# Cross attention with 16 heads over 1500 keys: spreading the reciprocal denominators by TensorE in every batch

## The reference, cut to what matters

```python
scores = einsum('bshd,bld->bhsl', q_latent, kv_r)   # 16 batches, 56 x 16 rows, 1500 keys
attn   = softmax(scores, axis=-1)
ctx_c  = einsum('bhsl,bld->bhsd', attn, kv_r)       # latent width 64
out    = folded_output_projection(ctx_c)
```

## Time and profile before

| | |
|---|---|
| device time, median of 3 executions | 3199.64 us |
| lowest and highest | 3179.69 and 3200.17 us |
| span of the profiled execution, first to last instruction | 3214.1 us |
| cross attention of layer 0, layer 1, layer 2 | 226 to 652, 1327 to 1751, 2300 to 2719 us of the span |

### The profile page before, as it was taken

How to read it: one execution, slowest core, us unless ns; L and a number is a source line. 1 busy time by engine, 2 the same in 40 slices (tenths; PEclk the granted TensorE clock), 3 DMA queues, 4 the chain that set the end, 5 groups by cost and what they waited for, 6 DMA issues and landing times. The chain is left out here.

```text
span 3214.1 us, 48214 instructions
## 1 busy us (share of the span) xinstructions
PE 2927.4 (91%) x17993; PEld 1703.9 (53%) x17997; DVE 1876.2 (58%) x3657; ACT 1245.7 (39%) x1997; POOL 873.8 (27%) x743
## 2 busy tenths in 40 slices
PE   4899999869999899899999989989899999677999
PEld 3755555545455463455556557753455555346444
DVE  6568888642222357778875143347788885654222
ACT  3456666511111242555554122222456554424221
POOL 4325555400343124333333000004333333211000
PEclk8899999979999899999999999999999999888999
DMA  1148898614122112377775010012367775001111
GB/s 32 53 124 179 177 181 172 135 29 134 35 105 92 52 43 78 88 152 171 168 148 138 11 42 25 26 43 78 77 154 165 153 167 134 15 12 24 39 40 33
DMA packets 221444, 299.25 MB, mean 93 GB/s; under 512 B 127178, under 2 KB 149052, under 8 KB 218764
## 3 DMA queue, kind: packets, MB, share of 16 engines
q1 hardware_dynamic: 220348, 294.39, 39.2%
q10 hardware_dynamic: 864, 1.77, 0.2%
HBM read 120.52 MB, written 21.38 MB: 44 GB/s over the span
## 5 line engine op out<-in xcount | busy, mean ns | idle before, releaser
L1796 ACT ACTIVATE l2x_shared<-l2x_shared,l2x_a_low 128x1500 f32<-128x1500 f32 x112 | 173.3, 1547 | 160.4 <-DVE l2x_shared L1748 156.5
L1796 ACT ACTIVATE l1x_shared<-l1x_shared,l1x_a_low 128x1500 f32<-128x1500 f32 x112 | 173.3, 1548 | 159.6 <-DVE l1x_shared L1748 156.1
L1796 ACT ACTIVATE l0x_shared<-l0x_shared,l0x_a_low 128x1500 f32<-128x1500 f32 x112 | 173.3, 1548 | 146.4 <-DVE l0x_shared L1748 145.7
L1660 PE MATMUL l0x_a_S_ps<-l0x_kt,l0x_a_q 64*128 64x366 f32 (+1 forms) x896 | 176.0, 507 | 3.5 <-DVE l0x_shared L1748 3.0
L1660 PE MATMUL l1x_a_S_ps<-l1x_kt,l1x_a_q 64*128 64x366 f32 (+1 forms) x896 | 178.6, 515 | 0.6 <-DVE l1x_shared L1748 0.6
L1660 PE MATMUL l2x_a_S_ps<-l2x_kt,l2x_a_q 64*128 64x366 f32 (+1 forms) x896 | 178.4, 515 | 0.6 <-DVE l2x_shared L1748 0.6
L2040 DVE TENSOR_TENSOR l0f_times_up<-l0f_gate,l0f_U 128x448 f32<-128x448 f32 x64 | 39.8, 621 | 236.9 <-PE l0f_U L1958 236.9
L2009 ACT ACTIVATE l0f_gate<-l0f_G 128x448 f32<-128x448 f32 x72 | 39.2, 545 | 310.7 <-PE l0f_G L1953 310.7
L1353 POOL TENSOR_TENSOR l2x_q_straight<-l2x_q_straight,l2x_q_crossed 128x448 f32<-128x448 f32 x48 | 54.5, 1136 | 339.6 <-DVE l2x_q_crossed L1344 339.6
L1695 PE MATMUL l1x_a_C_ps<-l1x_space,l1x_v 128*64 128x192 f32 (+1 forms) x1024 | 121.8, 373 | 21.7 <-DMA l1x_space<-l1x_a_blocks 18.9
L1695 PE MATMUL l2x_a_C_ps<-l2x_space,l2x_v 128*64 128x192 f32 (+1 forms) x1024 | 117.8, 363 | 20.8 <-DMA l2x_space<-l2x_a_blocks 17.2
(11 more groups left out here) (678 smaller groups left out, 6478.7 us busy)
## 6 DMA issues: line engine op xcount, KB each, us to landing
l0x_space<-normed SPq DMA_DIRECT2D x192, 128.0 KB
l1x_space<-normed SPq DMA_DIRECT2D x192, 128.0 KB
l2x_space<-normed SPq DMA_DIRECT2D x192, 128.0 KB
l0x_space<-l0x_a_blocks SPq DMA_DIRECT2D x186, 96.0 KB, 3.3
l1x_space<-l1x_a_blocks SPq DMA_DIRECT2D x186, 96.0 KB, 3.3
l2x_space<-l2x_a_blocks SPq DMA_DIRECT2D x186, 96.0 KB, 3.4
l0f_gu<-in_L_ffn_gu SPq DMA_DIRECT2D x36, 256.0 KB, 2.6
l0x_a_q<-l0x_qa SPq DMA_DIRECT2D x32, 224.0 KB
```

Of the source, the lines that this page charges most:

```text
L1660: last = pe.matmul(S_ps[:, 2 * pair + rows_, 0:w], q[lane, b % 2, k * 128:(k + 1) * 128], kt[lane, b % 2, pair * W1:pair * W1 + w], start= ...
L1796: act.activation(p[:, n % 2], p[:, n % 2], ACT.Exp, bias=low[:, n % 2, 1:2], scale=-1.0, accum_out=den[:, b % 2, k:k + 1]).then_inc(exp_re ...
```

## The change

The path through DRAM is gone, and every batch is normalised as the last one was. PE makes the 14 products at the ends of groups 0 and 1 of every batch; DVE multiplies `cn` in place, after tile k = 3 (group 0) and after tile k = 6 (group 1) of the next batch; POOL's scatter is a copy that waits for both; SP neither stores nor loads inverses. PE waits, before it starts a group of the next batch in its bank, until DVE has read the reciprocals out of it.

```diff
-                    if b > 0:
-                        fetch_inverses(b - 1)
...
                     move(sp, b, 1, range(4) if b + 1 < B else range(2))
-                    if b + 1 < B:
-                        store_inverses(b)
...
                 def scatter(b):
                     pool.wait_ge(kept_own, 8 * b + 12 if b + 1 < B else 8 * B)
-                    if b + 1 == B:
-                        pool.wait_ge(normed, 2)
-                        pool.tensor_copy(ct[:, :, b, 0:S], cn[:, b % 2].rearrange("c (s h) -> c h s", s=S)).then_inc(scattered, 1)
-                        return
-                    pool.wait_ge(c_kept, 2 * b + 2)
-                    pool.wait_ge(r_loaded[b % 2], 32 * (b // 2 + 1))
-                    pool.tensor_tensor(ct[:, :, b, 0:S], cn[:, b % 2].rearrange("c (s h) -> c h s", s=S),
-                                       rrow[:, b % 2].rearrange("c (s h) -> c h s", s=S), ALU.mult).then_inc(scattered, 1)
+                    pool.wait_ge(normed, 2 * b + 2)
+                    pool.tensor_copy(ct[:, :, b, 0:S], cn[:, b % 2].rearrange("c (s h) -> c h s", s=S)).then_inc(scattered, 1)
...
                         if b > 0:
                             pe.wait_ge(c_kept, 2 * (b - 1) + g + 1)
+                            pe.wait_ge(normed, 2 * (b - 1) + g + 1)
...
-                    if b + 1 == B:
-                        pe.wait_ge(rden_ready, B)
-                        for t in range(COUNT[g]):
...
+                    pe.wait_ge(rden_ready, b + 1)
+                    for t in range(COUNT[g]):
+                        k = FIRST[g] + t
+                        for odd in range(2):
+                            last = pe.matmul(C_ps[odd * CW:(odd + 1) * CW, g, 256 + t * 64:320 + t * 64],
+                                             rden[:, b % 2, k:k + 1].to_broadcast([128, CW]),
+                                             m.ident[:, odd * CW:(odd + 1) * CW], start=True, stop=True)
                     last.then_inc(valued, 1)
...
                 def invert(b):
 
                     if b > 1:
-                        dve.wait_ge(r_stored[b % 2], 16 * (b // 2))
+                        dve.wait_ge(valued, 2 * (b - 2) + 2)
                     dve.reciprocal(rden[:, b % 2], den[:, b % 2]).then_inc(rden_ready, 1)
...
                     if n + 2 < N:
                         negate(n + 2)
-                normalise(0)
-                normalise(1)
+                    if n % T in (3, 6) and n >= T:
+                        normalise(n // T - 1, n % T // 6)
+                normalise(B - 1, 0)
+                normalise(B - 1, 1)
```

More of the change, by code:

```diff
@@ L1440, in attend @@
     cn = ahead.shared[:, 2 * LK:2 * LK + C].rearrange("c (a n) -> c a n", a=2)
-    rrow = ahead.shared[:, 2 * LK + C:2 * LK + 2 * C].rearrange("c (a n) -> c a n", a=2)
     def group(k):
@@ L1478, in attend @@
         c_kept = st.sem(name + "c_kept")
-        r_stored = [st.sem(f"{name}r_stored{j}") for j in range(2)]
-        r_loaded = [st.sem(f"{name}r_loaded{j}") for j in range(2)]
         normed = st.sem(name + "normed")
@@ L1522, in store_keys @@
                     sp.dma_start(m.kt_dram[b], kt[:, b % 2]).then_inc(k_stored[b % 2], 16)
[L1524 to L1539, removed]
                 for b in range(2):
@@ L1768, in invert, with normalise @@
                     if b > 1:
-                        dve.wait_ge(r_stored[b % 2], 16 * (b // 2))
+                        dve.wait_ge(valued, 2 * (b - 2) + 2)
                     dve.reciprocal(rden[:, b % 2], den[:, b % 2]).then_inc(rden_ready, 1)
-                def normalise(g):
-                    b = B - 1
+                def normalise(b, g):
                     a, z = columns(g)
@@ L1858, in latent_cross @@
         m.kt_dram = nc.dram_tensor("kt_rotated", (B, 128, LK // 2), F32, kind="Internal").ap()
-        m.r_dram = nc.dram_tensor("inverses", (B, QT_TILES, 128), F32, kind="Internal").ap()
         ctx = d["ctx"], d["ctx_cos"], d["ctx_sin"]
```

## The result

Over twelve executions of each kernel the median is 3166.29 us, against 3191.97 us before. The ratio is 0.992, 95% interval 0.990 to 0.9941: 0.8% faster. Each kernel had one disturbed execution among its twelve (3478.8 us before, 3373.5 us after), which the medians hold and the ratio leaves out. The first three of the twelve executions of the kernel before had a median of 3199.64; all twelve together lie lower, and the other eleven spread from 3174.65 to 3205.99, while those of the changed kernel keep within 3157 and 3170.

A forecast was written before the change was run, and what follows sets the result against it. TensorE was taken to bound the steady loop, with irregular DMA waits besides. Profiled: 3214.1 + 49.5 (products) - 60 (relief) - 4 (last batches) = 3199.6 us; timed, the middle between 3185 and about 3200 gave 3193, range 3168 to 3230.

The forecast's parts named there:

- What bounds the kernel: Cross attention: TensorE is full in undisturbed batches (24.76 us in layer 1); late DMA moves add an irregular 71.1 us together.
- the price of the products: Ends of groups 0 and 1 on PE: 0.63 and 0.47 us, 1.10 us a batch, +49.5 us over 45 batches.
- wrong it would be if the undisturbed batch isn't 25.9 us: Sign in the profile after: undisturbed windows of layers 1 and 2 should last 25.86 us with PE full.
- The relief: PE's waits for moves and slow clock shrink: -60 us (bounds 35 and 71), with -4 us more in the last batches.
- The discount for timed executions: Profiled span against timed median: 14.5 us of delays may be missing in timed executions; the middle of both cases was taken.
- rival 2: All DMA delays go, the last batches' waits too: 3199.6 + 49.5 - 71 - 11 = 3167 us; chance 0.12.
- The cause: SP's store of inverses: small DRAM writes hold up transfers next to them; 3.5 KB took over 11 us to land.
- SP's queue: Without the two loads, 1.34 us of queue go, so moves of group 1 start at 1572.25 instead of 1573.59.
- The slack of 0.63 us: Group 0's products precede the tile needing the moves; with 1.34 us of queue, a late move has 2.0 us more.
- Rival 1: Moves stay late and products are paid: 3249 us without relief, 3226 with the 2 us of slack; chance 0.21.
- rival 4: VectorE becomes the bound through its two multiplications: up to +40 us, 3233 us; chance 0.04.
- Rival 3: Products run slower in PE's stream, 0.10 us a record: +126 us in place of +49.5, 3262 us; chance 0.03.

The follow-up runs named there:

- experiment 1: Changed kernel without the 14 products in batches 1 to 14 of each stage: 3131.4 us, ratio to the kernel before 0.9725.
- experiment 2: Changed kernel with the store of inverses in 4 B pieces put back behind the moves of group 1, read by nobody: 3191.0 us, ratio to the kernel before 0.9913.
- experiment 4: Changed kernel with the store put back at its old place as 128 pieces of 28 B, read by nobody: 3170.6 us, ratio to the kernel before 0.9845.
- experiment 5: Changed kernel with the 4 B store put back directly in front of the moves of group 0: 3230.9 us, ratio to the kernel before 1.0095.
- experiment 9: Changed kernel with the 4 B store back and two small loads of 7 rows of 512 B in the old loads' place: 3181.9 us, ratio 0.9941.
- experiment 8: Changed kernel with store and loads of inverses both back at their old places, read by nobody: 3206.6 us, ratio to the kernel before 1.0008.
- experiment 3: Changed kernel with both loads of inverses put back in every batch, the store only in each stage's first two batches: 3175.7 us, ratio 0.9869.

## Why the prediction missed

**What bounds the kernel** was right: a steady loop bound by TensorE, and an irregular cost from the moves. The forecast of a full PE in every batch, no wait for `normed`, DVE below PE and moves of group 1 issued earlier came true. DVE is busy 22.78 us in a batch of 25.58. POOL idles 9.7 us before its copy, in place of 12.5 before its multiplication; the copy comes right behind DVE's multiplication. The moves of group 1 start 1.4 us after the turn of tile k = 6 begins:

```profile
1528.84 0.35 DVE L1745 TENSOR_TENSOR l1x_shared<-l1x_shared,l1x_a_C_ps 128x192 f32<-128x192 f32 x1
...
1529.32 1.01 POOL L1578 COPY l1x_ct<-l1x_shared 128x448 f32<-128x448 f32 x1 [9.70 <-DVE l1x_shared L1745]
...
1550.85 0.70 PE L1643 MATMUL l1x_a_T_ps<-ident,l1x_shared 128*119 128x128 f32 x4
...
1552.23 1.18 SPq L1502 DMA_DIRECT2D l1x_space<-l1x_a_blocks  x2
```

In the kernel before the same turn began at 1570.37, and these moves 3.2 us after it, at 1573.59:

```profile
1570.37 0.70 PE L1673 MATMUL l1x_a_T_ps<-ident,l1x_shared 128*119 128x128 f32 x4
```

So they come 1.8 us earlier, where 1.3 was forecast.

**The step that failed is the price of the products**: "less than that I exclude". I read 0.63 us from the start of their loads to the start of the next loads, and took the next piece to be unchanged behind them. It isn't. The end of group 0 in the changed kernel:

```profile
1537.97 0.63 PEld L1666 LDWEIGHTS l1x_a_C_ps<-l1x_space,l1x_v 128*64 128x64 f32 x8 [0.51 <-issue]
...
1538.67 0.71 PEld L1677 LDWEIGHTS l1x_a_C_ps<-ident,l1x_a_rden 128*64 128x64 f32 x16
1538.88 0.64 PE L1677 MATMUL l1x_a_C_ps<-ident,l1x_a_rden 128*64 128x64 f32 x16
1539.29 0.20 PEld L1664 LDWEIGHTS l1x_a_C_ps<-l1x_space,l1x_v 119*64 119x64 f32 x4
...
1539.77 0.50 PEld L1643 LDWEIGHTS l1x_a_T_ps<-ident,l1x_shared 128*119 128x119 f32 x4 [0.28 <-issue]
```

and the same place in the kernel before:

```profile
1558.30 0.63 PEld L1695 LDWEIGHTS l1x_a_C_ps<-l1x_space,l1x_v 128*64 128x64 f32 x8 [0.51 <-issue]
...
1559.00 0.36 PEld L1693 LDWEIGHTS l1x_a_C_ps<-l1x_space,l1x_v 119*64 119x64 f32 x4
...
1559.64 0.50 PEld L1673 LDWEIGHTS l1x_a_T_ps<-ident,l1x_shared 128*119 128x119 f32 x4 [0.28 <-issue]
```

The products take their 0.62 us, from 1538.67 to 1539.29. But the four loads behind them take 0.20 us in place of 0.36, and the next turn comes 0.48 us after these loads began in place of 0.64: 0.16 us are given back. So group 0 costs 1.80 - 1.34 = 0.46 us from the first row to the last, group 1 by the windows 0.82 - 0.46 = 0.36, and 45 batches 36.9 us in place of 49.5. The prediction had named the sign itself: wrong it would be if the undisturbed batch isn't 25.9 us. It is 25.58.

**The relief** was sized at 60 + 4 us. Against the profiled execution all went: the span fell by 53.7 us with 36.9 us added, so 90.6 us of waits and slow clock are gone, 71.1 in the windows and 19.5 in the first and last batches and outside, where the prediction had put 4 for the last batches, and 11 at most. The medians give less: 25.7 + 36.9 = 62.6 us. The discount for timed executions was thus right in kind, and rival 2 (everything goes) is what happened in the profile. Its 3167 is the measured time within 1 us, but by luck: the products were 12.6 us cheaper than in its sum and the three executions it starts from 7.7 us too slow, and against that the medians gave 62.6 us of relief in place of its 82. With 36.9 for the products alone it would have been 3155.

The miss of 26.7 us against the forecast of 3193 is made up of 12.6 us for the products, 7.7 us by which the median of twelve executions of the kernel before is below that of three, and 6.4 us of relief (62.6, where the forecast had 3199.6 + 49.5 - 3193 = 56.1). The time lies only 2 us under the range, so without any one of the three it would have been inside. The products are the largest part, and the one that both the windows and experiment 1 show.

**The cause** I gave for the late moves was the store's small writes, as a reading that the trace didn't prove. Experiments 2, 4 and 5 show it for the part that the store plays: the same bytes in 28 B pieces cost 4 us, in 4 B pieces 25 us, and in 4 B pieces just ahead of other moves 65 us. What the prediction took as speaking against it, that the late move was issued before the store, is no objection: the late move is the store's direct neighbour in the queue, as the landings beside experiment 5 show. But it isn't the store alone: with the loads beside it, it costs more than both by themselves. By SP's queue, as the prediction had it (1.34 us earlier), nothing was won that experiment 9 could find, with about half of that time put back. The slack of 0.63 us in front of PE's use is there in the order of the work, and experiment 8 fits it; it would have saved some 20 us there, which wasn't tried by itself.

The Trainium skill, DMA: Bandwidth & Descriptors, section Specifications, asks for at least 512 B in a transfer. By the runs the store of 28 B pieces, also under that limit, costs some 4 us where the one of 4 B pieces costs 25, so here the limit alone doesn't tell what a store costs.

**Rivals.** Rival 1 (moves stay late) and rival 4 (VectorE) fell, by the windows. Rival 3, the slower products, fell the other way: from their start to the next start they take 0.62 us (0.63 in the tail), and the piece behind them gives 0.16 back.

## What to carry to other kernels

A DMA of few bytes in hundreds of 4 B pieces can cost much more than its bytes, and it is paid by its neighbours in the queue, in front of it and behind it. Turn the tile on TensorE first, so that the store has whole rows. When an instruction is put into a full TensorE stream, price it from the start of the piece in front of it to the end of the piece behind it, and let the price have a lower bound too. When a wait is irregular, look at the spread of the timed runs beside the profiled span before you count all of the profile's delays as won: here the profile gave 90.6 us of relief and the medians 62.6.

## What the runs showed of the hardware

- A store of 3.5 KB in 896 pieces took about 10 us to land (9.9 in experiment 3, over 11 in rows 8), and in 128 pieces 1.8 us. From some 4 us after it on, other transfers fell from about 200 GB/s to 82 and less for 4 us, with one DMA issue of SP held for 4.3 us. Why it is some us later and not at once stays open.
- The move issued directly ahead of such a store landed after 8.0 to 11.1 us in all ten batches of layers 1 and 2 in which PE waited for group 1, and within 3.7 us in the others.
- The store alone costs 28 us, the kernel with the loads alone 11 us (8.5 of them POOL's), and both at least 61 us (without products); with products it is 25, 9 and 41. What joins them wasn't settled.
- The product of seven weight columns with 128 moving columns (128 x 7 turned) takes 0.28 us as a record, with one load of 0.08 us.
